# Graph attention with residual and layer norm: x in 8 transfers, the attention vector as one row spread by TensorE, the eighth score matmul in the bank of the maximum, and ScalarE's scaling behind four relus

## The reference

```python
s_i = emb @ attn[:d]
s_j = emb @ attn[d:]
e = jax.nn.leaky_relu(s_i + s_j.T, negative_slope=0.2)
e = e + jnp.where(adj > 0, 0.0, -1e9)
alpha = jax.nn.softmax(e, axis=1)
# with emb = x:
x = _layernorm(x + alpha @ emb, axis=-1)
```

## Time and profile before

| | |
|---|---|
| median of 3 runs | 267.31 us (265.73 to 268.03) |
| the profiled execution | 265.73 us |
| its span, first to last instruction | 263.8 us |
| PE busy | 247.7 us, 94% |
| DVE busy | 236.4 us, 90% |
| ACT busy | 171.9 us, 65% |
| DMA | 71.73 MB, mean 272 GB/s |
| mean granted TensorE clock | 0.989 |

### The profile page before, as it was taken

The page is one execution under the profiler, slowest core; times in us unless marked ns, Lnnn a source line. Parts: engine busy times, 40 slices in busy tenths (PEclk is TensorE's granted clock), DMA queues, the critical chain, the costliest instruction groups (busy, mean ns, idle before and its releaser), DMA issues.

```text
span 263.8 us, 5316 instructions
## 1 busy us (share of the span) xinstructions
PE 247.7 (94%) x2113; PEld 240.3 (91%) x2113; DVE 236.4 (90%) x378; ACT 171.9 (65%) x247; POOL 37.5 (14%) x78
## 2 busy tenths in 40 slices
PE   4796999999999999999999999999999999999980
PEld 4544999999999999999999999999999999999870
DVE  0779989999999999999998999899998999999952
ACT  0589998555985568754864588555964497569410
POOL 3000000000051003300230003300330014000622
PEclk9997999999999999999999999999999999999998
DMA  5999999999999999999999999999999999960011
GB/s 154 313 347 302 306 308 313 309 318 314 317 316 335 306 286 297 297 338 295 281 257 348 289 286 298 326 314 292 301 314 322 282 287 284 343 197 2 16 25 42
DMA packets 70362, 71.73 MB, mean 272 GB/s; under 512 B 2992, under 2 KB 68784, under 8 KB 70336
## 3 DMA queue, kind: packets, MB, share of 16 engines
q1 hardware_dynamic: 34624, 34.67, 47.7%
q10 hardware_dynamic: 34624, 34.67, 47.0%
q0 software_dynamic: 1088, 2.03, 2.5%
HBM read 69.27 MB, written 2.10 MB: 271 GB/s over the span
## 4 chain that ended last, share of the span: by engine, by line
DMA 74%; DVE 8%; ACT 5%; ACTq 4%; PE 4%; issue 2%; POOL 1%; DVEq 0%
DMA adj_in<-in_adj_dram 71%; DVE weights L630 6%; ACTq L240 3%; DMA x_raw<-in_x_dram 3%; ACT q_row L357 2%; PE psum L742 2%; ACT mask_bytes L377 2%; PE psum L727 1%; DVE mask_t L525 1%; ACTq L223 1%; PE psum L716 1%; POOL out_dram L248 1%; ACT xj L369 1%; DVE x_raw L575 0%; ACT x_raw L434 0%
## 5 line engine op out<-in xcount | busy, mean ns | idle before, releaser
L742 PEld LDWEIGHTS psum<-xj,weights 128*128 128x128 f32 x2048 | 230.1, 193 | 2.9 <-DVE weights L630 1.8
L742 PE MATMUL psum<-xj,weights 128*128 128x129 f32 x2048 | 230.9, 276 | 0.9 <-DVE weights L630 0.8
L630 DVE SCALAR_TENSOR_TENSOR weights<-q_row,r_j,mask_t 128x512 f32<-128x512 f32 x256 | 171.2, 741 | 0.1
L377 ACT ACTIVATE mask_bytes<-adj_in,sig_bias 128x4096 uint8<-128x4096 int32 x30 | 111.3, 3709 | 64.2 <-DMA adj_in<-in_adj_dram 64.2
L525 DVE STREAM_TRANSPOSE mask_t<-mask_bytes 128x1024 uint32<-128x1024 uint32 x31 | 38.5, 1241 | 8.6 <-ACT mask_bytes L377 8.4
L303 POOL TENSOR_SCALAR neg_mean<-total 128x4 f32<-128x4 f32 x7 | 1.5, 214 | 179.8 <-ACT x_raw L385 179.8
L312 POOL DMA_DIRECT2D out_dram<-x_raw x28 | 14.5, 521 | 22.2 <-ACT x_raw L399 22.0
L399 ACT ACTIVATE x_raw<-x_raw,offset,rstd 128x128 f32<-128x128 f32 x28 | 11.5, 479 | 2.8 <-POOL offset L309 2.8
L392 ACT ACTIVATE unused<-x_raw,neg_mean 128x128 f32<-128x128 f32 x28 | 10.9, 390 | 2.4 <-POOL neg_mean L303 2.4
L497 DVE TENSOR_TENSOR adj_in<-x_raw,attn_j 128x1024 f32<-128x1024 f32 x4 | 4.8, 1221 | 7.9 <-DMA attn_j<-in_L_gnn_attn_dram 7.6
L727 PE MATMUL psum<-adj_in,attn_iw 128*128 128x512 f32 x16 | 9.0, 665 | 2.8 <-ACT q_row L357 2.8
(11 more groups left out here) (58 smaller groups left out, 59.5 us busy)
## 6 DMA issues: line engine op xcount, KB each, us to landing
adj_in<-in_adj_dram SPq DMA_DIRECT2D x64, 512.0 KB, 10.0
adj_in<-in_adj_dram ACTq DMA_DIRECT2D x64, 512.0 KB, 12.4
out_dram<-x_raw POOLq DMA_DIRECT2D x28, 64.0 KB, 5.3
x_raw<-in_x_dram SPq DMA_DIRECT2D x8, 128.0 KB, 5.5
x_raw<-in_x_dram ACTq DMA_DIRECT2D x8, 128.0 KB, 6.2
out_dram<-x_raw POOLq DMA_DIRECT2D x4, 32.0 KB, 1.9
attn_j<-in_L_gnn_attn_dram POOLq DMA_DIRECT2D x1, 64.0 KB, 6.3
out_dram<-x_raw SPq DMA_DIRECT2D x4, 16.0 KB, 1.9
```

The lines of the kernel that those rows point to most:

```text
L377: nc.scalar.activation(mask_bytes[:, g % BYTE_SLOTS, :, :, :], adj_in[:, g % ADJ_SLOTS, :, :, :], ACT.Sigmoid, bias=sig_bias[:], scale=200 ...
L630: nc.vector.scalar_tensor_tensor(weights[:, slot_of(n, c), :], q_row[:, n * BANK:(n + 1) * BANK], r_j[:, c:c + 1], mask_t[:, (n * PIECES + ...
L742: return nc.tensor.matmul(banks[(n * K + t) % 8][:, 0:D1], weights[:, slot_of(n, c), t * P:(t + 1) * P], xj[:, c, 0:D1], start=(c == 0), s ...
```

## The change

Three things are edited. x comes in 8 transfers of 256 KB (two parts of 16 tiles in place of four stripes of 8). attn comes in one POOL transfer as a row of 256 numbers in one partition; two PE matmuls with a row of ones spread its second half over the partitions (`attn_j`, bank 0) and turn its first half into the wide column (`attn_iw`, bank 1), and DVE copies both out of PSUM. The ones are now set by DVE. PE's 14 busy transposes write bank 0 and stand behind the first copy. The eighth score matmul goes to bank 0, where the maximum was, waits for that maximum to be read, and is issued sixth. ACT loads piece 1 behind the fourth copy instead of the second, and does relus 0, 1, 2 and 7 ahead of `scale_xj(0)`.

The diff, without the declarations and without the part that loads everything again:

```diff
@@ constants
-    S_I_BANK = [3, 2, 1, 4, 5, 6, 7, 4]
-    S_I_ORDER = [0, 3, 1, 2, 4, 5, 6, 7]
+    ATTN_J_BANK = 0
+    ATTN_I_BANK = 1
+    S_I_BANK = [3, 2, 1, 4, 5, 6, 7, 0]
+    S_I_BY_PE = [0, 1, 2, 3, 4, 7, 5, 6]
+    S_I_ORDER = [0, 1, 2, 7, 3, 4, 5, 6]
+    X_PARTS = 2
+    XC = CHUNKS // X_PARTS
@@ load_x, called for each part by SP and ACT
-                queue.dma_start(x_raw[B * q:B * (q + 1), st * SC:(st + 1) * SC, :].rearrange("b (f k) d -> b f (k d)", k=K),
-                                x_v[q, :, st * SC // K:(st + 1) * SC // K, :]).then_inc(x_loaded[st], 16)
+                queue.dma_start(x_raw[B * q:B * (q + 1), part * XC:(part + 1) * XC, :].rearrange("b (f k) d -> b f (k d)", k=K),
+                                x_v[q, :, part * XC // K:(part + 1) * XC // K, :]).then_inc(x_loaded[part], 16)
@@ gpsimd
-            pool.dma_start(attn_j[:], attn[D:2 * D, :].rearrange("d o -> o d").broadcast_to([P, D])
-                           ).then_inc(attn_j_loaded, 16)
-            pool.dma_start(attn_i[:], attn[0:D, :]).then_inc(attn_loaded, 16)
+            pool.dma_start(attn_row_in[:], attn[:, :].rearrange("d o -> o d")).then_inc(attn_loaded, 16)
@@ scalar
-                if m == 1:
+                if m == 3:
                     load_piece(act, HIGH_HALF, 1)
-                if m == 2:
-
-                    act.wait_ge(products_ready, S_J_BY_ACT + 1)
+
+                    act.wait_ge(products_ready, 2)
...
             s_i_piece(0)
             q_factors(0, 1)
+            load_piece(act, HIGH_HALF, 2)
+            for rb in S_I_ORDER[1:4]:
+                s_i_piece(rb)
             scale_xj(0)
-            s_i_piece(S_I_ORDER[1])
-            load_piece(act, HIGH_HALF, 2)
-            for rb in S_I_ORDER[2:]:
+            for rb in S_I_ORDER[4:]:
                 s_i_piece(rb)
@@ vector
-            dve.wait_ge(attn_j_loaded, 16)
-            for st in range(STRIPES):
-                dve.wait_ge(x_loaded[st], 16 * Q)
...
-                    nc.vector.tensor_scalar(attn_iw[:], ones[:], attn_i[:], None, ALU.mult).then_inc(attn_wide, 1)
...
+            nc.vector.memset(ones[:], 1.0).then_inc(ones_ready, 1)
+            dve.wait_ge(attn_j_in_psum, 1)
+            nc.vector.tensor_copy(attn_j[:], banks[ATTN_J_BANK][:, 0:D]).then_inc(attn_j_ready, 1)
+            dve.wait_ge(attn_i_in_psum, 1)
+            nc.vector.tensor_copy(attn_iw[:], banks[ATTN_I_BANK][:, 0:P]).then_inc(attn_wide, 1)
+            dve.wait_ge(attn_j_ready, 1)
+            dve.wait_ge(x_loaded[0], 16 * Q)
+            product_of(0)
+            sum_products(0)
+            product_of(S_J_BY_ACT)
+            dve.wait_ge(x_loaded[1], 16 * Q)
+            product_of(2)
+            product_of(3)
+            sum_products(2)
+            sum_products(3)
@@ tensor
+            pe.wait_ge(ones_ready, 1)
+            pe.wait_ge(attn_loaded, 16)
+            nc.tensor.matmul(banks[ATTN_J_BANK][:, 0:D], ones[0:1, :], attn_row_in[:, D:2 * D],
+                             start=True, stop=True).then_inc(attn_j_in_psum, 1)
+            nc.tensor.matmul(banks[ATTN_I_BANK][:, 0:P], attn_row_in[:, 0:D], ones[0:1, :],
+                             start=True, stop=True).then_inc(attn_i_in_psum, 1)
             pe.wait_ge(consts_ready, 1)
+            pe.wait_ge(attn_j_ready, 1)
             for _ in range(WARM):
                 nc.tensor.transpose(banks[MAX_BANK][:, 0:P], ident[:], ident[:])
...
-                if rb == RB - 1:
-                    pe.wait_ge(s_i_ready, S_I_ORDER.index(S_I_BANK.index(bank)) + 1)
+                if bank == MAX_BANK:
+                    pe.wait_ge(max_found, 1)
...
-            for rb in range(4, RB):
+            for rb in S_I_BY_PE[4:]:
                 s_i_piece(rb)
```

More of the change, by code:

```diff
@@ L138, in gat_kernel @@
         banks = [psum[:, i, :] for i in range(8)]
-        x_loaded = [sem(f"x_loaded{st}") for st in range(STRIPES)]
-        attn_j_loaded = sem("attn_j_loaded")
+        x_loaded = [sem(f"x_loaded{part}") for part in range(X_PARTS)]
         attn_loaded = sem("attn_loaded")
@@ L259, in _ @@
         def _(sp):
-            for st in range(STRIPES):
-                load_x(sp, LOW_HALF, st)
+            for part in range(X_PARTS):
+                load_x(sp, LOW_HALF, part)
             for g in range(ALL_PIECES):
@@ L332, in _ @@
         def _(act):
-            for st in range(STRIPES):
-                load_x(act, HIGH_HALF, st)
+            for part in range(X_PARTS):
+                load_x(act, HIGH_HALF, part)
             load_piece(act, HIGH_HALF, 0)
@@ L491, in sum_products, with product_of @@
                 nc.vector.reduce_sum(s_j[:, c], prod[:, c, :], X).then_inc(s_j_ready, 1)
-            dve.wait_ge(attn_j_loaded, 16)
-            for st in range(STRIPES):
-                dve.wait_ge(x_loaded[st], 16 * Q)
+            def product_of(st):
                 c = slice(st * SC, (st + 1) * SC)
```

24 lines of the change are left out of this document (11 added, 13 removed).

## The result

| | before | after |
|---|---|---|
| median, same chip | 266.3 us (265.4 to 268.03, 6 runs) | 269.54 us (268.62 to 269.98, 6 runs) |
| ratio, 95% interval | | 1.010 [1.0054, 1.0145] |
| the profiled execution, its span | 265.73, 263.8 us | 269.41, 267.3 us |
| mean granted TensorE clock | 0.989 | 0.977 |

The change makes the kernel 1.0% slower, 2.7 to 3.7 us. The forecast was 1.1 us faster, and its range ended at 268.5. Some runs of a kernel lie far above the rest (before on one chip: 264.6 to 274.5 us, and two of 372.5 and 661.5), so medians here are over all runs, while ratios leave out runs that are more than 1.5% above the kernel's fastest, except where the text says otherwise.

A forecast was written before the change was run, and what follows sets the result against it. The prediction took the DMA stream of adjacency landings to bound the kernel, PE next with 1.2 us of slack. The stream's 1.1 us gain, other edits at nothing, took the median 267.31 to 266.2 us; range 264.3 to 268.5.

The forecast's parts named there:

- attn over PE: Kernel start: attn row lands at 4.8 us, transpose for the maximum follows 12.2 us later, at 17.0, 0.4 later than before.
- What 0.4 us does: VectorE's start on piece 0: at 18.0 us, 0.7 earlier, so the stream's 1.1 us counts in full.
- The four relus ahead: Before the first product: reordered relus and the eighth matmul in bank 0 cost nothing, hidden by DVE's work to 30.9.
- The DMA stream at the start: From 3.5 to 6.5 us: removing POOL's two attn transfers returns 1.1 us of stream, bounds -0.3 and 1.64.
- So the end is the DMA stream's: Kernel's end: adjacency landings set it, so an earlier stream can move everything; PE is next, with 1.2 us of slack.
- The attn row is late, and PE sets the end: Rival, chance 0.15: row lands at 7.3, maximum at 19.5, PE 1.8 to 2.2 late, end 0.6 to 1.0 later, 268.3 us.

The follow-up runs named there:

- attn row alone: Kernel before with attn loaded as one row and spread by TensorE, nothing else of the change: 268.85 us, ratio 1.013.
- joined versions: Changed kernel, row on SP's queue, ScalarE's issues moved earlier, piece 3's among the last relus; the second also with the old relu order: 265.71 and 265.56 us.
- relu order alone: Kernel before with only the eighth score matmul in bank 0 and four relus ahead of the scaling: 268.0 us, ratio 1.001.
- piece 2 late: Kernel before with ScalarE's half of piece 2 issued behind the relus: 274.68 us, ratio 1.032; profiled execution 269.23 us.
- kept busy: Changed kernel with 30 more identity transposes on PE between the last score matmul and the first product: 272.01 us, ratio 1.021.
- x in two parts alone: Kernel before with x in 8 transfers of 256 KB, attn by POOL as it was: 268.24 us, ratio 1.007.

## Why the prediction was wrong

- **"attn over PE"** failed in one term. The landing was taken at 4.8 with the bounds 3.7 and 7.3; it was 6.8. The sum behind it held: 12.2 us from landing to the transpose for the maximum, measured 19.05 - 6.8 = 12.25. So the maximum came at 19.05 and not at 17.0. The same row landed at 4.8 in the kernel with the attn row alone, where x comes in 16 transfers, and between 6.6 and 7.2 in the six profiles with the row on POOL and x in 8. So the value was not wrong as such: it depends on how x is loaded beside it. The second of the rules that the prediction drew from the Trainium skill, page "DMA: Bandwidth & Descriptors" (Queues, rings and completion order), by which the increment lands behind earlier writes, agrees: the row that is issued on SP ahead of x landed at 2.1 us. That run doesn't tell the order apart from the change of queue.
- **"What 0.4 us does"** fell with it: VectorE turned to piece 0 at 19.96, not at 18.0.
- **"The four relus ahead"** was costed at nothing, and for the start of the products that holds (joined versions, 265.71 and 265.56). But the step was priced by what waits for the relus and the scaling only. ScalarE's sequencer also issues the high halves of pieces 2 and 3 behind this work; these were not in the sum, though with the late maximum they went from 18.76 to 21.16 and from 25.87 to 29.45. The same issues now stand in front of the relus that the first product waits for, and hold ScalarE's engine there (1.27 us at 21.16).
- **"The DMA stream at the start"** was right in its mechanism: the dip went (319 and 306 GB/s against 157 where the two transfers are gone, 154 where they stay, in the relu order alone). Its price for piece 1's later issue, "0.3 us of loss, a guess", is the worst term. The step held that the queue was still on piece 0 at the issue. It was (issue 13.73; the queue's last packets of piece 0 move between 15.0 and 15.5); but data did not flow at the issue, and up to 19 us not a packet of piece 1's half came. The landing of piece 0 at 18.71, by which the step judged the queue, is that of both halves. In piece 2 late a delay of 4.6 us on another piece alone moved PE's end by 3.5 us in the profiled execution.
- **"So the end is the DMA stream's"** was half true. A stream that starts earlier gains nothing if TensorE cannot use it, and the chain of before did not show that PE was as near. The slack of 1.2 us was worked out from 11 records per microsecond in one window; over 72 to 120 us PE does 9.0. By that the slack is (27 - 20) / 9.0 = 0.8 us. No kernel of the study is told from before on the faster side, not even those that keep 345 GB/s to 40 us and have the maximum in place (the lowest ratio is 0.998 [0.995, 1.002]).
- The rival **"The attn row is late, and PE sets the end"** (0.15) is the mechanism of half of it, with a maximum at the 19.5 that it names and a first product of 26.3 (26.70). Its price, 0.6 to 1.0, was too low: the slack was smaller, the first six chunks took about 8.5 us at the low clock and not 6.4 (26.3 to 32.7), and the late maximum also held ScalarE's issues. (Whether the clock alone was worth its 1.7 isn't shown: kept busy, PE waits for weights instead.) The other half, the queues, stood among no rivals.

## What to carry to other kernels

Where two queues share a stream, price every moved instruction on an engine that also issues transfers by the issues behind it. Ask when each half's first packets are wanted, and issue it ahead of that by what the trace shows between issue and packets (over 5 us here); a faster start of the stream makes the same issue late. Price too what the issue does to the engine that makes it, since its work waits behind it. And an earlier end of one bound is worth only the slack of the next one, measured over a long stretch.

## What was not expected of the hardware

- One queue alone moves 209 to 213 GB/s, two move 348, with the engines' busy share the same (1.12 and 1.10). A packet of the lone queue takes 16 x 3 x 1.126 / 629 = 86 ns, one of the two takes 50.
- An issue is far ahead of its data while the other queue is busy: after, piece 1's half is issued at 13.73, none of its packets moves up to 19 us, and 112 do between 19 and 20. At the start the fastest transfer of x was down in 2.4 us.
- Once out of step the queues can stay so for a long time, since a piece's landing needs both halves and both queues wait for it: 273 GB/s from 56 to 72 us in x in two parts alone, with 11 records of PE lost. It is not always so: after is back at 314 GB/s in that stretch, and runs in step to 40 us fall out of it too (272 and 275 GB/s), without loss on PE.
- PE's wait of 3.71 us in piece 2 late, up to 41.40, was paid for twice: the granted clock is 0.89 from 40 to 56 us, where before has 1.00 and no such wait.
- The cause of the dip is only half settled. Taking the two POOL transfers away ends it in two kernels (319 and 306 GB/s); with them in place and x in two parts it moves, to 156 and 127 GB/s between 6 and 7 us. But with the row on SP's queue there is a flat one, 232 to 250 GB/s in four kernels, with no transfer of POOL at all. Its cause stays open.
